# Two heads' attention scores in the two row halves of the TensorE array, and a new order at the group ends of a state space scan

## The reference

```python
# Mamba-2 layer: 128 heads of 64 channels in 8 groups (INNER = 8192)
M = einsum('bcihn,bcjhn->bcijh', C, B) * L                 # L = exp(segment sums), within a chunk
Y = einsum('bcijh,bcjhp->bcihp', M, hid_dt) + carried states
yg = (Y + D * hid) * silu(gate)
y = yg * rsqrt(mean of squares over each group of 1024 channels + eps) * gnorm_w
out = residual + y @ out_proj_w.T                          # 8192 -> 512
# attention
logits = einsum('bhqd,bhkd->bhqk', rope(q), rope(k)) / sqrt(16), causal
out = softmax(logits) @ v, then @ Wo.T
```

## Time and profile before

| | before |
|---|---|
| median of 3 runs (lowest, highest) | 2547.78 us (2546.03, 2548.27) |
| profiled execution | 2546.22 us, span 2544.4 us |
| instructions | 32506 |
| busy: PE, PEld, DVE, ACT, POOL | 93%, 72%, 65%, 52%, 52% |
| mean granted TensorE clock | 0.974 |

### The profile page before, as it was taken

One profiled execution on the slowest core, in us unless ns is written; L12 is line 12 of the kernel. 1 busy time (PEld: TensorE's weight loads), 2 busy tenths in 40 slices (PEclk: granted clock), 3 DMA queues, 4 the chain that ended last, 5 costly groups with the idle time before them and its releaser, 6 DMA issues. The chain is left out here.

```text
span 2544.4 us, 32506 instructions
## 1 busy us (share of the span) xinstructions
PE 2370.6 (93%) x12122; PEld 1828.5 (72%) x12122; DVE 1665.9 (65%) x2163; ACT 1314.6 (52%) x1902; POOL 1329.2 (52%) x875
## 2 busy tenths in 40 slices
PE   6997899999999999999999999999779986989986
PEld 5875688788788788778778778878668763555643
DVE  5555787687588588588578578678455525574424
ACT  3214576477477467467567567657423223325533
POOL 2221498598499489489579669759622210000000
PEclk9998899999999999999999999999889998999998
DMA  5321333233233233233223333323124302000001
GB/s 133 96 73 57 104 114 104 86 98 114 75 111 114 79 94 109 88 101 111 86 90 110 100 90 110 98 79 109 54 71 102 100 14 77 2 2 2 2 2 47
DMA packets 163260, 203.98 MB, mean 80 GB/s; under 512 B 24380, under 2 KB 86080, under 8 KB 162976
## 3 DMA queue, kind: packets, MB, share of 16 engines
q1 hardware_dynamic: 163104, 201.90, 26.2%
HBM read 198.37 MB, written 3.15 MB: 79 GB/s over the span
## 5 line engine op out<-in xcount | busy, mean ns | idle before, releaser
L1883 POOL TENSOR_TENSOR mamba_w_lo<-mamba_raw,mamba_w_hi 128x512 fp32r<-128x512 f32 x272 | 435.1, 1608 | 311.0 <-ACT mamba_w_hi L1711 311.0
L76 PE MATMUL psum<-mamba_hT_lo,mamba_w_hi 128*128 128x512 f32 x1152 | 461.9, 401 | 3.0 <-DVE mamba_bc L1974 3.0
L77 PE MATMUL psum<-mamba_hT_hi,mamba_w_hi 128*128 128x512 f32 x1152 | 456.2, 396 | 0.0
L78 PE MATMUL psum<-mamba_hT_hi,mamba_w_lo 128*128 128x512 f32 x1152 | 456.0, 396 | 0.0
L1902 POOL TENSOR_SCALAR mamba_L<-mamba_A,mamba_ts 128x256 f32<-128x256 f32 (+1 forms) x256 | 335.0, 1322 | 0.1
L2006 DVE TENSOR_TENSOR mamba_L<-mamba_L,mamba_cb 128x1536 f32<-128x1536 f32 x128 | 310.2, 2423 | 22.1 <-ACT mamba_L L1760 14.3
L1974 DVE SCALAR_TENSOR_TENSOR mamba_hid<-psum,mamba_cw,mamba_hid 128x1022 f32<-128x1022 f32 (+2 forms) x192 | 245.2, 1277 | 19.4 <-ACT mamba_hid L1718 14.9
L76 PEld LDWEIGHTS psum<-mamba_hT_lo,mamba_w_hi 128*128 128x128 f32 x1152 | 216.9, 188 | 53.3 <-DVE mamba_bc L1974 3.3
L78 PEld LDWEIGHTS psum<-mamba_hT_hi,mamba_w_lo 128*128 128x128 f32 x1152 | 216.9, 188 | 52.5
L77 PEld LDWEIGHTS psum<-mamba_hT_hi,mamba_w_hi 128*128 128x128 f32 x1152 | 217.1, 188 | 49.1
L2033 DVE SCALAR_TENSOR_TENSOR mamba_zs_lo<-mamba_z,mamba_dgn,mamba_zs_hi 128x512 fp32r<-128x512 f32 x128 | 117.2, 921 | 175.1 <-ACT mamba_zs_hi L1783 175.1
(11 more groups left out here) (278 smaller groups left out, 4988.9 us busy)
## 6 DMA issues: line engine op xcount, KB each, us to landing
mamba_A<-mamba_a_dram SPq DMA_DIRECT2D x128, 512.0 KB, 4.7
mamba_raw<-in_win SPq DMA_DIRECT2D x144, 256.0 KB, 2.6
mamba_raw<-in_wout SPq DMA_DIRECT2D x128, 256.0 KB, 2.6
mamba_Eb<-mamba_e_dram SPq DMA_DIRECT2D x128, 128.0 KB, 3.0
ffn_raw<-in_w SPq DMA_DIRECT2D x80, 128.0 KB, 3.6
ffn_scl<-in_s SPq DMA_DIRECT2D x80, 128.0 KB, 3.7
ffn_scl<-in_s SPq DMA_DIRECT2D x86, 64.0 KB, 2.3
ffn_raw<-in_w SPq DMA_DIRECT2D x20, 256.0 KB, 2.6
```

Of the source, the lines that this page charges most:

```text
L76: e.matmul(out, wh, ml, start=start, stop=False)
L77: e.matmul(out, wh, mh, start=False, stop=False)
L78: return e.matmul(out, wl, mh, start=False, stop=stop)
L1883: e.tensor_tensor(w.lo[:, k % NSPLIT, :], raw[:, k % NRAW, :], w.hi_read[:, k % NSPLIT, :], ALU.subtract).then_inc(s["w_lo"], 1)
```

## The change

In attention, `score` and `score_t` use only the 64 rows of a head (`HALVES`) instead of all 128, so that the matmuls of two key heads stand in the two row halves. `score_t(t, m)` now makes two key heads at once, into banks 4 and 5, and waits until both exponentials before it are done. The mask of the diagonal is added from 64 rows too, in two products per head with half of the query columns each (`halfm`, a second copy of the mask, loaded by two more DMAs and rounded by one more copy on ScalarE). The units `score` between them are spread over two places in a quad instead of four. `score` keeps its 128-row mask products.

In the scan, the last part of each half counts `out_done` bank by bank instead of `out_used` once; `outputs` waits for each bank by itself. `turn_b` (TensorE) and `turned_b` (ScalarE) move from ahead of the second half to behind its second part. On VectorE the second `masked` and the first `products` come ahead of `z_low(grp, 1, 2)`, the second `products` right behind it.

```diff
@@ -840,6 +841,7 @@
     ROWS, ONE, SPARE = 32, AHD, 48
+    HALVES = (slice(0, P // 2), slice(P // 2, P))
     SCALE = AHD ** -0.5
@@ -852,8 +854,9 @@
         cos, sin, rot = c.sb("cos", [P, SEQ]), c.sb("sin", [P, SEQ]), c.sb("rot", [P, P])
-        cmask = c.sb("cmask", [P, P])
+        cmask, hmask = c.sb("cmask", [P, P]), c.sb("hmask", [P, 2, P])
         maskr, identr = c.sb("maskr", [P, P], F32R), c.sb("identr", [P, P], F32R)
+        halfm = c.sb("halfm", [P, 2, P], F32R)
         sel = c.sb("sel", [P, 2, QPK + NKV, P], F32R)
@@ -864,6 +867,9 @@
                 e.dma_start(cmask[:], d["causal_add"]).then_inc(sel_in, 16)
+                for h in range(2):
+                    e.dma_start(hmask[HALVES[h]], d["causal_add"].rearrange("(n p) k -> p n k", n=2)
+                                ).then_inc(sel_in, 16)
                 for dst, src in ((wk, "wk"), (wq, "wq"), (wv, "wv"), (wo, "wo")):
@@ -871,7 +877,7 @@
-                e.wait_ge(sel_in, 32)
+                e.wait_ge(sel_in, 64)
                 for half in range(2):
@@ -881,6 +887,7 @@
                 e.copy(maskr[:], cmask[:]).then_inc(mask_ready, 1)
+                e.copy(halfm[:], hmask[:]).then_inc(mask_ready, 1)
                 e.copy(identr[:], ident[:]).then_inc(mask_ready, 1)
@@ -1017,8 +1024,8 @@
                     for h in range(2):
-                        e.matmul(psum[:, 2 * (k % 2) + h, 0:n], qs[:, b, z, qt * P:(qt + 1) * P],
-                                 ks[:, b, 2 * (z // QPK) + h, 0:n], start=True, stop=False)
+                        e.matmul(psum[:, 2 * (k % 2) + h, 0:n], qs[HALVES[h], b, z, qt * P:(qt + 1) * P],
+                                 ks[HALVES[h], b, 2 * (z // QPK) + h, 0:n], start=True, stop=False)
                     for h in range(2):
@@ -1029,20 +1036,25 @@
-                def score_t(t, i):
+                def score_t(t, m):
+
...
                     b, qt = STEPS[s]
-                    kv, k = 4 * j + i, 4 * t + i
-                    if k >= 2:
-                        e.wait_ge(exped, k - 1)
-                    if i == 0 and (j, kt) == (0, 0):
+                    k = 4 * t + 2 * m
+                    if k:
+                        e.wait_ge(exped, k)
+                    if m == 0 and (j, kt) == (0, 0):
                         e.wait_ge(m_in[s % 2], 64 * (s // 2 + 1))
-                    q = qs[:, b, QPK * (kv // 2):QPK * (kv // 2 + 1), qt * P:(qt + 1) * P]
-                    out = ps[4 + k % 2].rearrange("p (h q) -> p h q", h=QPK)
-                    last = e.matmul(out, ks[:, b, kv, kt * P:(kt + 1) * P], q, start=True, stop=kt < qt)
-                    if kt == qt:
-                        last = e.matmul(out, maskr[:], identr[:, :].unsqueeze(1).to_broadcast([P, QPK, P]),
-                                        start=False, stop=True)
+                    z = QPK * (2 * j + m)
+                    outs = [ps[4 + h].rearrange("p (h q) -> p h q", h=QPK) for h in range(2)]
+                    for h in range(2):
+                        last = e.matmul(outs[h], ks[HALVES[h], b, 4 * j + 2 * m + h, kt * P:(kt + 1) * P],
+                                        qs[HALVES[h], b, z:z + QPK, qt * P:(qt + 1) * P], start=True, stop=kt < qt)
+                    for n in range(2 if kt == qt else 0):
+                        for h in range(2):
+                            last = e.matmul(outs[h][:, :, HALVES[n]], halfm[HALVES[h], n, :],
+                                            identr[HALVES[h], HALVES[h]].unsqueeze(1).to_broadcast([P // 2, QPK, P // 2]),
+                                            start=False, stop=n == 1)
                     last.then_inc(scored_t, 1)
@@ -1114,9 +1126,9 @@
                     units = units_at(t) if t < TQ else []
-                    for i in range(4 if t < TQ else 0):
-                        score_t(t, i)
-                        for k in range(i * len(units) // 4, (i + 1) * len(units) // 4):
+                    for m in range(2 if t < TQ else 0):
+                        score_t(t, m)
+                        for k in range(m * len(units) // 2, (m + 1) * len(units) // 2):
                             score(*units[k])
@@ -1156,7 +1168,7 @@
                     k = 4 * t + i
-                    e.wait_ge(scored_t, k + 1)
+                    e.wait_ge(scored_t, k // 2 + 1)
                     if k >= NPT:
@@ -1368,7 +1380,7 @@
                  "sub_a", "sub_p", "exped", "m_ready", "state", "prev_ready", "y_done", "o_done", "skipped", "yo_ready",
-                 "combined", "gated", "squared", "added", "rstd_ready", "z_hi", "z_lo", "out_used", "out_read", "dve")
+                 "combined", "gated", "squared", "added", "rstd_ready", "z_hi", "z_lo", "out_used", "out_done", "out_read", "dve")
         s = {n: c_.sem(n) for n in names}
@@ -1401,6 +1413,11 @@
+
+        def taken(q):
+
+            n, i = divmod(q, GT)
+            return (s["out_done"], 4 * (n + 1)) if i == GT - 1 else (s["out_used"], n * (GT - 1) + i + 1)
@@ -1609,7 +1626,10 @@
                                        w.lo[:, k % NSPLIT, :], i == 0, i == GT - 1)
-                    last.then_inc(s["out_used"], 1)
+                        if i == GT - 1:
+                            last.then_inc(s["out_done"], 1)
+                    if i < GT - 1:
+                        last.then_inc(s["out_used"], 1)
@@ -1690,9 +1710,10 @@
                         inner(grp + 1, 1)
-                        turn_b(grp + 1)
                     for i in range(GT):
                         out_part(grp, 1, i)
+                        if more and i == 1:
+                            turn_b(grp + 1)
@@ -1779,12 +1800,12 @@
                     if q >= 2:
-                        e.wait_ge(s["out_used"], q - 1)
+                        e.wait_ge(*taken(q - 2))
                     e.activation(zs.hi[:, q % 2, :], z[:, i, p, :], ACT.Copy, scale=dgn[:, grp, i, 1:2]
...
                 def after_part(grp, p, i):
-                    e.wait_ge(s["out_used"], part(grp, p, i) + 1)
+                    e.wait_ge(*taken(part(grp, p, i)))
                     split(plan.tile["o", grp, p, i] + 4)
@@ -1867,12 +1888,12 @@
                             silu("C", grp + 1)
-                    if more:
-                        turned_b(grp + 1)
                     for i in range(GT):
...
                         after_part(grp, 1, i)
+                        if more and i == 1:
+                            turned_b(grp + 1)
@@ -2039,11 +2060,11 @@
                 def outputs(grp, p):
-                    e.wait_ge(s["out_used"], part(grp, p, GT - 1) + 1)
                     e.wait_ge(s["rstd_ready"], grp + 1)
...
                         n = p * 4 + t
+                        e.wait_ge(s["out_done"], 8 * grp + n + 1)
                         e.scalar_tensor_tensor(x[:, n, :], ps[4 + t], rstd[:, n:n + 1], x[:, n, :], ALU.mult, ALU.add
@@ -2165,16 +2186,13 @@
                         masked(grp + 1, 0)
+                    if more:
+                        products(2 * u + 2)
+                        masked(grp + 1, 1)
                     z_low(grp, 1, 2)
                     if more:
-                        products(2 * u + 2)
-                    z_low(grp, 1, 3)
-                    if more:
-                        masked(grp + 1, 1)
-                    z_low(grp, 1, 4)
-                    if more:
                         products(2 * u + 3)
-                    for i in range(5, GT):
+                    for i in range(3, GT):
                         z_low(grp, 1, i)
```

## The result

| | before | after |
|---|---|---|
| median (lowest, highest) | 2547.8 us (2544.7, 2549.6), 20 runs | 2565.1 us (2544.5, 2575.3), 20 runs |
| profiled execution | 2546.22 us, span 2544.4 | 2568.36 us, span 2566.5 |
| mean granted TensorE clock | 0.974 | 0.949 |

The change makes the kernel slower, by 0.6%: after over before is 1.0056, 95% interval 1.0037 to 1.0076. The forecast was 24 us faster; the time lies outside its range, on the other side. The new kernel's runs also spread over 31 us, and they line up with the granted clock: 0.959 to 0.962 goes with 2544.5 to 2555.1 us, 0.951 to 0.954 with 2561.0 to 2566.8 us, 0.948 to 0.950 with 2568.2 to 2575.3 us.

A forecast was written before the change was run, and what follows sets the result against it. The scan was taken as bound by TensorE's waits and instruction count, attention by a chain of TensorE and ScalarE. Scan -29.7, loop +5.2, prologue +0.5 sum to -24.0 us: median 2524 us, range 2512 to 2541.

The forecast's parts named there:

- The scan's sum: Scan: four terms, 13.3 + 5.6 + 7.7 + 3.1, make 29.7 us less; lower bound about 25.
- steps 1 and 3: Scan group ends: `turn_b`'s wait for `masked` goes, 13.3 us; the next group's wait for the first add goes, 7.7 us.
- Step 2: Scan, inside half 1: TensorE's wait for a `z_low` goes and no other replaces it, 7 x 0.8 = 5.6 us.
- The rival that part 1.2 starves: Scan: `z_low` 1.2 comes too late under the new order, costing up to 19 us, total 2543; 7%.
- The chain of a quad: Attention: second pair 1.67 us after the first; start to `weigh` 2.65 us in tile 3, 3.24 in tile 2 with three units.
- The change of shape: Attention: switching between 64-row and 128-row matmuls costs 0.2 us each, one inside each unit and one behind it.
- The loop's sum: Attention loop: waiting for both banks and shape changes outweigh the saving, +5.2 us over query tiles 3 to 0.
- the range's upper end (+14): Attention loop: about +14 us if the change of shape costs twice as much as assumed.
- slow-clock rival: Attention: TensorE streams fewer columns at a time, so the clock falls to 0.5; +109 us, 2633; 5%.
- "nothing" for the 32 units: Units ahead of the loop: no time change, as VectorE paces them at 1.14 us each, TensorE's part taking 0.9.
- +2.4 us for a slow quad: Attention loop: at granted clock 0.5, TensorE's share of about 3 us doubles with 0.6 us slack.
- slower than before from about ten quads on: Attention loop: number of quads at the slow clock from which the new kernel would be slower than the old one.

The follow-up runs named there:

- scan_only: The changed kernel with only the scan's edits kept, attention as in the kernel before; 2518.9 us, ratio 0.9884 to the kernel before.
- full_rows: The changed kernel with all attention scores and masks read from 128 rows again, the wait for both exponentials kept; 2548.7 us, ratio 1.0004.
- filler_half: The changed kernel plus one unused 512-column product read from 64 rows per unit ahead of the loop; 2556.7 us, ratio 1.0056.
- same_half: The changed kernel with both heads read from the upper 64 rows, so they can't run side by side (second head's scores wrong); 2699.7 us, ratio 1.0593.
- filler: The changed kernel plus one unused product of 128 rows and 512 columns behind each unit ahead of the loop; 2547.8 us, ratio 1.0002.
- loop_filler: `filler` with one more such 128-row product ahead of each of the loop's 80 pairs; 2587.9 us, ratio 1.0167.
- units_full: The changed kernel with the units (`score`) from 128 rows again, the loop's pairs left in halves; 2538.4 us, ratio 0.9963.

## Why the prediction was wrong

**The scan's sum held**: 31.4 us in the trace against 29.7; `scan_only`, with the same scan, has 28.3 in its trace and 28 as a median, so traces differ by 3 us here. The waits for `masked` and for the first add went, as steps 1 and 3 say. Step 2's "no wait replaces this one" is off by a little: 1.3 us in seven waits remain. It gave the `z_low` of part 1.3 0.7 us; it took 1.78 (468.39 to 470.17), and TensorE needed it at 469.97. The trace of before has this in the same place, in a row that the prediction didn't use:

```profile
471.82 1.79 DVE L2033 SCALAR_TENSOR_TENSOR mamba_zs_lo<-mamba_z,mamba_dgn,mamba_zs_hi 128x512 fp32r<-128x512 f32 x1
```

Why it takes longer there stays open. The rival that part 1.2 starves didn't happen: `z_low` 1.2 was done by 465.7, 1.4 us ahead of the part's start at 467.09.

**The chain of a quad held**: 1.67, 2.65 and 3.24 us are 1.68, 2.65 and 3.28, and the halves run together. The change of shape was sized well in sum (0.39 against 0.40), though not evenly: 0.09 us into the 64-row shape and 0.30 out of it, 0.11 of that inside the mask, whose weight loads start with it (2279.17) where those of `full_rows` start 0.17 us ahead of it.

**The loop's sum was mis-sized**: +5.2 forecast (its first term is a slip: twelve quads at 0.05 make 0.6, not 0.4), about +11 measured at full clock. By query tile 3 to 0, forecast and measured: +0.4, 3.8, 0.4, 0.6 and +3.6 (1.9 of it the slow quad 1), 5.8, 2.1, 1.3. The plain quads of tile 3 are within 0.06 us; what I left out are the quads that also hold a step's transposes, +0.2 to 0.34 each, where one quad was taken as the pattern for sixteen. It is inside the range's upper end (+14) and would by itself have left the kernel some 18 us faster.

**The step that failed is the slow-clock rival's "Against it: the clock stays 1.00 ahead of the loop, where VectorE paces TensorE", and the 5% that it led to.** The earlier trace rows shows a clock that holds with TensorE 80% busy, but every product in that row fills 128 rows. I read it as evidence on gaps and used it for a kernel whose products fill 64. What the runs showed in its place: with 64-row products the clock fell to 0.50 from 5.6 us into the units on, for 51.2 us, and for 130 us of attention in all, which costs some 40 us. The row was also weaker than it looked, since `scan_only` shows a fall under the same code. No row of before that I read has sparse 64-row work, so it couldn't speak against the rival; the honest reading was that the trace leaves it open. For the same reason "nothing" for the 32 units failed: they cost 7.4 us, and one way to see it coming was that TensorE's part, 0.9 us at full clock by the prediction, passes VectorE's 1.14 at half clock.

The rival's path was right, a slow clock that doubles TensorE's share, but not its reason, that TensorE streams fewer columns at a time: the clock also fell where the columns came without a gap (`filler_half`) and one product behind the other (`same_half`). Its price was nearly right in the loop: +2.4 us for a slow quad forecast; quads 27 to 30 are 13.2 us longer than `filler`'s, 3.3 each. Ahead of the loop it was +0.4 forecast per unit and 7.4 / 32 = 0.23 measured. Its extent was too large: 12 or so of 40 quads are slow, not all, so 2565 and not 2633. Its bound, "slower than before from about ten quads on", is about where the result lies.

What stays open: why the loop's falls differ from run to run (`filler` 2535.5 to 2574.9 us), why a 128-row product per pair didn't hold the clock there, and what distinguishes, within the loop, a 64-row stretch at which the clock falls from one where it holds. In after it held, but for one dip of 3 us, for 102.4 us from 2253.5, though the products are of the same kind.

## What to carry to other kernels

A saving of array rows isn't only worth its matmul time: 64-row products can lower the granted clock, and here 130 us at 0.50 (some 40 us lost) took back more than all scan waits had given. Before moving fp32 scores into row halves, ask whether TensorE's time is what bounds the stage; here it wasn't, and keeping 128 rows with zeros in the other half (`scan_only`) was free and 46 us faster. A clock level read in the old profile is evidence only for the kind of instruction that it was read under, and one trace is one draw of it.

## What the runs showed of the hardware that I had not expected

- 64-row products were followed by a fall of the clock even with TensorE busy 100% of the time (`filler_half`) and when not side by side (`same_half`: 126.3 us at 0.50); one 128-row product added per unit held it at 1.00 in the units. The same remedy in the loop didn't (`loop_filler`: 0.85).
- 128-row units alone don't hold it either: `scan_only`, `full_rows` and `units_full` have 0.90 or 0.91 there, a fall of 6.8 us each.
- Two row halves run together at no cost: 496 ns for each, and for both. The Trainium skill (TensorE: Matmul & The Clock Gate, Part 3, Measured speedup vs the span model) has a shortfall for four row tiles; for two, no row here shows one.
- The price of leaving the 64-row shape (0.30 us) is some three times that of entering it (0.09), by the estimate above.
- A scheme of waits that frees two banks together instead of one by one, with the units in two places instead of four, cost 22.6 us in a loop of 215, with the same matmuls.
